# A table of expert tiles in two parts, the first worked out from seven of eight batches

## The reference

```python
def _L0_ffn_ref(hidden_states, router_w, router_b, w1, b1, w2, b2):   # E = 16 experts, K = 4
    logits = hidden_states @ router_w + router_b
    probs = jax.nn.softmax(logits, axis=-1)
    topw, topi = jax.lax.top_k(probs, K)
    topw = topw / jnp.sum(topw, axis=-1, keepdims=True)
    combine = jnp.sum(jax.nn.one_hot(topi, E) * topw[..., None], axis=2)
    ...
    def body(acc, expert):
        hmid = jax.nn.gelu(x @ w1e + b1e, approximate=False)          # w1e 256x512, w2e 512x256
        return (acc + (hmid @ w2e + b2e) * ce[:, None], None)
x = x + _L0_attn_ref(_layernorm(x), ...)
x = x + _L0_xattn_ref(_layernorm(x), ctx_1024, ctx_1024, ...)
x = x + _L0_ffn_ref(_layernorm(x), ...)
```

## Time and profile before

| what | value |
|---|---|
| median of 3 runs | 1757.58 us (1753.62 to 1761.1) |
| the profiled execution | 1751.44 us |
| its span, first to last instruction | 1749.4 us |
| mean granted TensorE clock | 0.968 of full speed |
| TensorE busy | 1597.4 us (91%) |
| VectorE, ScalarE, GpSimd busy | 1185.3, 1069.6, 505.0 us |
| the expert block starts, in the span | 1225.05 us |

### The profile page before, as it was taken

The page is one execution under the profiler, slowest core; times in us unless marked ns, Lnnn a source line. Parts: engine busy times, 40 slices in busy tenths (PEclk is TensorE's granted clock), DMA queues, the critical chain, the costliest instruction groups (busy, mean ns, idle before and its releaser), DMA issues. The chain is left out here.

```text
span 1749.4 us, 35493 instructions
## 1 busy us (share of the span) xinstructions
PE 1597.4 (91%) x12466; PEld 1341.6 (77%) x12466; DVE 1185.3 (68%) x2648; ACT 1069.6 (61%) x2698; POOL 505.0 (29%) x431
## 2 busy tenths in 40 slices
PE   5899889999999999999999999961699999999995
PEld 4888867677777776776777777741699999999995
DVE  6988856667677677776776776655566666666662
ACT  4555466666666566666666666642466666666663
POOL 2444400000301202103013021044155554554544
PEclk9999999999999999999999999985799999999997
DMA  3121110000100201101002001074577777877873
GB/s 96 37 85 73 37 61 1 1 25 1 64 25 14 75 1 45 45 1 65 25 6 84 1 29 36 1 256 166 155 163 181 173 175 176 177 179 164 188 171 46
DMA packets 92622, 144.52 MB, mean 83 GB/s; under 512 B 12272, under 2 KB 50720, under 8 KB 92448
## 3 DMA queue, kind: packets, MB, share of 16 engines
q1 hardware_dynamic: 61824, 101.40, 18.6%
q0 software_dynamic: 28896, 38.62, 12.2%
q10 hardware_dynamic: 1728, 2.23, 0.4%
HBM read 90.76 MB, written 51.46 MB: 81 GB/s over the span
## 5 line engine op out<-in xcount | busy, mean ns | idle before, releaser
L1193 ACT ACTIVATE xa_prob<-xa_S,xa_nmax 128x512 f32<-128x512 f32 (+3 forms) x512 | 266.5, 535 | 136.1 <-DVE xa_nmax L1303 124.8
L1710 POOL DMA_INDIRECT out<-ex_y,ex_x x158 | 254.6, 1611 | 262.7 <-ACT ex_y L1659 147.6
L1615 PE MATMUL ex_H<-ex_xT,ex_w 128*128 128x256 f32 x1896 | 247.3, 287 | 8.5 <-DVE ex_xT L1679 8.5
L1615 PEld LDWEIGHTS ex_H<-ex_xT,ex_w 128*128 128x128 f32 x1896 | 233.1, 192 | 8.9 <-issue 8.9
L1627 PE MATMUL ex_Y<-experts_w_hi,ex_hT 128*128 x1264 | 234.2, 279 | 0.0
L1515 POOL DMA_INDIRECT expert_rows<-xa_xn,xa_rows x128 | 127.8, 999 | 302.9 <-DVE xa_prob L1315 254.0
L1303 DVE TENSOR_REDUCE xa_nmax<-xa_S 128x2 f32<-128x1024 f32 (+3 forms) x256 | 198.1, 816 | 9.4 <-remote 8.2
L1627 PEld LDWEIGHTS ex_Y<-experts_w_hi,ex_hT 128*128 128x128 f32 x1264 | 198.9, 188 | 0.0
L1685 DVE TENSOR_TENSOR ex_hT<-ex_h,ex_hT 128x512 fp32r<-128x512 f32 x158 | 109.5, 694 | 122.7 <-ACT ex_hT L1652 87.5
L1207 ACT ACTIVATE xa_probT<-xa_work 128x512 f32<-128x512 f32 x256 | 140.0, 602 | 79.0 <-PE xa_work L1075 78.6
L1627 PE MATMUL ex_Y<-experts_w_lo,ex_hT 128*128 x632 | 176.8, 280 | 0.0
(11 more groups left out here) (312 smaller groups left out, 3583.8 us busy)
## 6 DMA issues: line engine op xcount, KB each, us to landing
ex_w_raw<-in_w SPq DMA_DIRECT2D x79, 512.0 KB
ex_x<-expert_rows SPq DMA_DIRECT2D x79, 273.0 KB
experts_w_lo<-in_w SPq DMA_DIRECT2D x4, 2048.0 KB, 9.7
expert_rows<-ahead_x SPq DMA_DIRECT2D x16, 273.0 KB
a_x<-in_x SPq DMA_DIRECT2D x8, 512.0 KB, 4.6
x_rows<-a_x_both SPq DMA_DIRECT2D x8, 512.0 KB, 5.4
ahead_ctx<-in_ctxT SPq DMA_DIRECT2D x8, 512.0 KB, 4.3
out<-xa_x SPq DMA_DIRECT2D x8, 512.0 KB
```

What stands on the lines that cost most here:

```text
L1193: m = act.activation(prob[n % 2][:, odd, PROB_AT[i]:PROB_AT[i] + width], SB[slot[at]][:, odd, col:col + width], ACT.Exp, bias=nmax[n % 2][ ...
L1615: m = pe.matmul(bank[:, (f % 2) * ROWS:(f % 2 + 1) * ROWS], ww[:, c, f * P:(f + 1) * P], xx[:, c, :], start=(i == 0), stop=(i == len(terms ...
L1710: pool.indirect_dma_start(out, bass.IndirectOffsetOnAxis(x_in[j % NX][:, a, ID:ID + 1].bitcast(I32), 0), y[j % NY][:, a, :], None, compute ...
```

## The change

The table is worked out in two parts. The first uses the counts of seven batches: only full tiles, and of them the first 41, a number that is there whatever the routing (`SURE_TILES`). It is computed in the last pair of the attention. The second holds the other 38 tiles and is computed in the expert block behind tile 4. Twelve of the last batch's sixteen scatters and the pads (now in halves) move into the expert block. x has five buffers instead of six, three of them tiles of the attention. The constants and buffers of the attention are kept through the expert block. The high parts of w2 are all made ahead of the output projection, and six of the low parts in the expert block.

```diff
+SURE_TILES = -(-((B - 1) * S * TOPK - E * (ROWS - 1)) // ROWS)
+LATE_TILES = MOE_TILES - SURE_TILES
@@ class Tables (new), part 0 and part 1
+    def work_out(self, dve, w, done, part, ahead, kept, count):
+        dve.memset(one, 1.0) ...
+        dve.tensor_scalar(self.scr_i[:], count[:], float(part * (ROWS - 1)), None, add)
+        ... shift right, to float; part 1: tiles = tiles - kept.used
+        ... scan, hit, owner, before; part 1 also some, behind, here, used (the tiles an expert has had)
+        dve.tensor_tensor(row, number[:], before, op=sub)
+        for back, meets in ((1, meets_1), (2, meets_2)):
+            dve.tensor_scalar(meets, row, float(back - 1), float(ADD_STEP), ALU.is_le, mult)
+        if part == 1: row = row + used
+        ... first row of the tile; part 0: kept.used = tiles of each expert, cut at SURE_TILES
+    def transpose(self, pe, w, done, bank, ident):
+        w.wait_ge(done, done.order[-5])
+        ... 4 transposes
+    def give_out(...): ... owner, first_row, landed of this part's tiles
@@ attention_plan
+        elif p == 7:
+            second.append(("tables", None))
...
-    plan += [*(("scatter", (b - 1, i, end, 1)) for i, _ in SCATTER_AT[1]), ("add_b2", (b - 1, 1)), *split_w2(0, 3),
-             ("output", (b, 1, 0)), *split_w2(3, 5), ("output", (b, 1, 1)), ("find3", b), ("norm3", b),
-             ("transpose_x3", (b, 0)), ("transpose_x3", (b, 1)), *split_w2(5, 9), ("route", b), ("choose", b), ("mark", b),
-             ("weigh_gates", b), ("place", b), *(("scatter", (b, i, end, 1)) for i in range(SCATTERS)),
-             ("tables", None), ("turn_gates", b), ("add_b2", (b, 0)), ("add_b2", (b, 1)), *split_w2(9, E)]
+    plan += [*(("scatter", (b - 1, i, end, 1)) for i, _ in SCATTER_AT[1]), ("add_b2", (b - 1, 1)),
+             *(("high_w2", e_) for e_ in range(E)), *low_w2(0, 3), ("output", (b, 1, 0)), *low_w2(3, 5), ("output", (b, 1, 1)),
+             ("first_loads", None), ("find3", b), ("norm3", b), ("transpose_x3", (b, 0)), ("transpose_x3", (b, 1)),
+             *low_w2(5, LOW_W2), ("route", b), ("choose", b), ("mark", b), ("weigh_gates", b), ("place", b), ("turn_gates", b),
+             *(("scatter", (b, i, end, 1)) for i in range(SCATTERS_FIRST)), ("add_b2", (b, 0)), ("add_b2", (b, 1))]
@@ cross_attention, sync
-                    ... 16 pad writes
+                elif step == "first_loads":
+                    w.wait_ge(t_dve, ("landed", 2))
+                    ... x and w1 of tiles 0 and 1 loaded by the first table
             w.wait_ge(x2_out, B - 1)
-            w.wait_ge(padded, E - 1)
+            for i, load in enumerate(first_in):
+                w.wait_ge(load, i % 2)
@@ cross_attention, gpsimd
-            w.wait_ge(scattered, (B - 1, *last_scatter))
@@ experts
-NX, NW = 6, 3
+NX, NW, FIRST = 5, 3, 2
-        x_in = [sb(f"x{i}", [P, RT, PAY]) for i in range(NX)]
+        x_in = [*kept.x_in, sb("x2", [P, RT, PAY]), xn3[:, 0:RT, :], xn3[:, RT:2 * RT, :]]
-        plan = [("load_x", j) for j in range(4)] + [("load_w1", j) for j in range(NW)]
-        plan += [("split_w1", 0), ("split_w1", 1), ("load_w1", NW), ("transpose", 0)]
+        plan = [("load_w1", 2), ("load_x", 2), ("split_w1", 0), ("transpose", 0), ("split_w1", 1), ("load_w1", 3), ("low_w2", None)]
         for j in range(MOE_TILES + 1):
+            plan += [("load_x", 3)] if j == 0 else []
             plan += [(step, at) for step, at in (("load_w1", j + 4), ("load_x", j + 4), ("transpose", j + 1), ("hidden", j),
                                                  ("split_w1", j + 2), ("results", j - 1)) if 0 <= at < MOE_TILES]
+            plan += [("tables", None)] if j == 4 else []
+            plan += [("pad", e_) for e_ in (2 * (j - 5), 2 * (j - 5) + 1) if 0 <= e_ < E]
@@ experts, sync
                 if step == "load_x":
+                    w.wait_ge(scattered[0], (B - 1, RT - 1, TOPK - 1), j == 3)
+                    w.wait_ge(scattered[1], last_scatter, j == 4)
+                    w.wait_ge(t_dve, ("landed", 2), j >= SURE_TILES)
+                    w.wait_ge(padded, (E - 1, RT - 1), j >= SURE_TILES)
                     w.wait_ge(t_pe, j - NX, j >= NX)
                     w.wait_ge(y_ev, j - NX, j >= NX)
-                    w.wait_ge(added[j % NY], (j - NX, RT - 1), j >= NX)
+                    w.wait_ge(added[(j - NX) % NY], (j - NX, RT - 1), j >= NX)
+                elif step == "pad":
+                    row = sp.value_load(pad_i[0:1, j:j + 1], min_val=0, max_val=E * REGION - ROWS)
+                    for a in range(RT):
+                        sp.dma_start(... half a pad ...)
@@ experts, tensor
+                if step == "tables":
+                    w.wait_ge(x_hi, 4)
+                    w.wait_ge(x_lo, 4)
+                    tables.transpose(pe, w, t_dve, XB[0], ident).then_inc(tables_pe.of(0), 1)
                 elif step == "transpose":
+                    w.wait_ge(t_dve, ("landed", 2), j == 6)
                 elif step == "results":
+                    w.wait_ge(low_w2, E - 1)
@@ experts, scalar
+            act.activation(warm[:], ahead.number[:], ACT.Gelu)
@@ experts, vector
+                if step == "low_w2":
+                    for e_ in range(LOW_W2, E):
+                        ... low part of w2 of expert e_
+                elif step == "tables":
+                    dve.tensor_tensor(pad_i[:], routing["count"][0:1, :], ahead.region[:], op=ALU.add)
+                    tables.work_out(dve, w, t_dve, 1, ahead, kept, routing["count"])
+                    w.wait_ge(tables_pe, 0)
+                    tables.give_out(dve, t_dve, 1, XB[0], ahead, routing)
@@ experts, gpsimd
-            ... ident
+            for i in range(SCATTERS_FIRST * ALL_ROWS // SCATTERS, ALL_ROWS):
+                ... the other twelve scatters
+            ... the pad's memset and iota
```

More of the change, by code:

```diff
@@ L791 @@
 PLACE = ("pos", "count", "key", "key_masked", "key8")
-TABLES = ("pad", "one", "tiles_up", "tiles_i", "tiles", "cum", "hit", "owner", "hit_tiles", "before", "some",
-          "owner_some", "row", "row_used", ("meets", 1), ("meets", 2), "row_up", "row_at", "row_past", "row_some", "owner_out", "row_out",
-          ("landed", 1), ("landed", 2))
 ROUTING = {"route": ROUTE, "choose": CHOOSE, "mark": MARK, "weigh_gates": WEIGH, "place": PLACE}
-SCATTERS, ALL_ROWS = 8, N_TILES * TOPK
+SCATTERS, ALL_ROWS, SCATTERS_FIRST = 8, N_TILES * TOPK, 2
 SCATTER_AT = {7: ((0, 3), (1, 2), (2, 1)), 0: ((3, 3), (4, 2), (5, 1)), 1: ((6, 3), (7, 2))}
@@ L886, in cross_attention @@
         pos = small("pos")
-        pads = x1[0][:].rearrange("p t c -> p (t c)")[:, 0:RT * PAY].rearrange("p (a c) -> p a c", c=PAY)
         gates, gatesT = sb("gates", [P, N_TILES, P], F32R), sb("gatesT", [P, S], F32R)
-        rows_i = [sb(f"rows{i}", [P, N_TILES, TOPK], I32) for i in range(2)]
+        rows_i = kept.rows_i
+        tables = Tables(sb, lg)
         heads = ExitStack()
@@ L944, in cross_attention @@
         lg_pe, pos_pe, tables_pe = signal("lg_pe", batches), signal("pos_pe", batches), signal("tables_pe", [0])
-        r_dve = signal("r_dve", [(at, n) for step, at in plan for n in ROUTING.get(step, ())] + list(TABLES))
+        r_dve = signal("r_dve", [(at, n) for step, at in plan for n in ROUTING.get(step, ())])
+        t_dve = signal("t_dve", Tables.of_part(0))
+        first_in = landed("first_x0", [0]), landed("first_x1", [1]), landed("first_w0", [0]), landed("first_w1", [1])
         r_act, r_rows = signal("r_act", batches), signal("r_rows", batches)
-        scattered = landed("scattered", [(b, t, k) for b in batches for t in range(N_TILES) for k in range(TOPK)])
-        padded = landed("padded", range(E))
+        scattered = landed("scattered", [(b, t, k) for b in batches[:-1] for t in range(N_TILES) for k in range(TOPK)])
+        scattered_last = [landed(f"scattered_last{u}", [(B - 1, t, k) for t in range(u * RT, (u + 1) * RT) for k in range(TOPK)])
+                          for u in range(N_TILES // RT)]
         last_scatter = (N_TILES - 1, TOPK - 1)
@@ L1429, in vector @@
                 elif step == "tables":
-                    tiles, cum, one, hit = (scr[:, i, :] for i in range(4))
-                    owner, before, row, some, meets_1, meets_2 = (of_tile[:, i:i + 1] for i in range(6))
-                    w.wait_ge(r_dve, (B - 1, "count"))
-                    dve.tensor_tensor(pad_i[:], count[0:1, :], region[:], op=ALU.add).then_inc(r_dve.of("pad"), 1)
-                    dve.memset(one, 1.0).then_inc(r_dve.of("one"), 1)
-                    dve.tensor_scalar(scr_i[:], count[:], float(ROWS - 1), None, ALU.add).then_inc(r_dve.of("tiles_up"), 1)
@@ L1481, in gpsimd @@
+                    tables.work_out(dve, w, t_dve, 0, ahead, kept, routing["count"])
+                    w.wait_ge(tables_pe, 0)
+                    tables.give_out(dve, t_dve, 0, bank(step, at), ahead, routing)
         def gpsimd(pool):
@@ L1526, in cross_attention, with experts @@
             block.sync(sync)
```

(11 more changed lines are left out.)

265 lines of the change are left out of this document (163 added, 102 removed).

## The result

| | before | after |
|---|---|---|
| median of 4 runs each, same chip | 1755.95 us | 1806.23 us (1796.25 to 1808.82) |
| the profiled execution | 1751.44 us | 1796.25 us |
| its span | 1749.4 us | 1794.5 us |

The ratio is 1.0273, with a 95% interval of 1.0234 to 1.0313: the change makes the kernel slower by 2.7%. Forecast were 1786.5, a range of 1759 to 1806 and a chance of 0.80 for slower. The direction was right; the cost was put too low. The measured ratio, taken on the 1757.58 that the forecast started from, is 1805.6: the very end of the range, and outside the 1773 to 1801 that the forecast gave its own mechanism. The medians differ by 50.3 and the spans of the two profiled executions by 45.1, where the prediction's sum was +29.

What follows compares the result with a forecast made beforehand. TensorE, busy 91% of the span, was taken as the bound. Seam -20, tiles 3 to 10 +13, 10 to 41 +12, 41 to 60 +14, 60 to 78 +8, end -2, pads +4: +29, 1786.5 us (1759 to 1806).

Steps and rivals of the forecast that it cites:

- The seam: Between attention and experts, to tile 3's transposes: the expert block starts earlier, in all -20 us (-28 to -13).
- Tiles 3 to 10: Early expert block: TensorE stands still 9.5 us for the second table behind tile 4; +13 us (+2 to +16).
- The pace of the ring: Expert stage: with five x buffers loads come late, 6.53 us a tile; tiles 10 to 41 +12 us (0 to +21).
- the three changes of expert: Tiles 10 to 41: each change of expert was given 0.6 us, five of them counted in that stretch.
- Tiles 41 to 78: Late expert stage: many first tiles of experts, then five-buffer pace; +14 us to tile 60, +8 us after.
- The chain through GpSimd: Tiles 41 to 60: an expert's first tile waits for earlier adds, 7.8 us a step, second tiles 3.7.
- 1: Expert stage: the five x buffers refill in time and cost nothing; -11 us, 1747 us; chance 0.09.
- 2: Expert stage: half the five-buffer cost, 6.27 us a tile; about 1760 us; chance 0.11.
- 4: Between attention and experts: something still holds block one, -5 us instead of -20; 1801 us; chance 0.03.
- 3: Expert stage: w1 loads also come late behind blocked x loads on SyncE, 6.8 us a tile; 1806 us; chance 0.05.

Runs made afterwards that it cites:

- e4: The changed kernel with TensorE's transposes for the second table issued a tile behind VectorE's steps, five x buffers: 1806.69 us, 1.0272 of the kernel before.
- e1: The kernel before with one edit, five x buffers instead of six: 1813.98 us, 1.0313 of the kernel before.
- e2: The changed kernel with a sixth x buffer from tile 20 on: 1771.66 us, 1.0079 of the kernel before.
- e5: The changed kernel with six x buffers from the first tile on: 1742.15 us, 0.9979 of the kernel before.
- e3: The changed kernel with the first table moved behind four of the last pair's eight turns, five x buffers: 1801.27 us, 1.0239 of the kernel before.
- e8: The changed kernel with the pad writes beside tiles 20 to 27 instead of 5 to 12, five x buffers: 1788.77 us, 1.0262 of the kernel before.
- e6: e5 with both table moves, those of e3 and e4, added: 1734.62 us, 0.9941 of the kernel before.
- e7: e6 with 17 sure tiles instead of 41: 1728.53 us, 0.9921 of the kernel before.

## Why the prediction was nearly right, point by point

**The seam** came out as forecast, -20.9 for -20, but by luck, as a sum of misses that cancel. The last pair and what follows, in the kernel after, against the earlier trace rows; TensorE, the four lines being the table's transposes, the weighing of the pair before, that of the last pair, and the output projection.

```profile
1154.68 1.01 PE L201 MATMUL xa_work<-ahead_ident,xa_of_tile 128*1 128x128 f32 x4 [7.07 <-DVE kept_used L196]
...
1155.62 3.28 PE L1196 MATMUL xa_work<-xa_probT,xa_v 128*64 128x512 f32 x16
...
1168.73 4.54 PE L1196 MATMUL xa_work<-xa_probT,xa_v 128*64 128x512 f32 x16 [6.47 <-ACT xa_probT L1310]
...
1174.95 0.55 PE L1213 MATMUL xa_work<-xa_Wo_hi,xa_oT_lo 128*128 128x256 f32 x1 [0.96 <-DVE xa_oT_lo L1436]
```

Count from the last pair's first scatter (1148.33 before, 1145.81 after), for the second profile had been 2.5 ahead already, which nothing in the change does. The first weighing is then 9.81 behind it instead of 1.62 ('s 1149.95): 8.2 late, and I had said 8.3. The last weighing is 12.9 late. Of the 8.3 I let 5 reach the block's end, and 11.7 did: the projection, at 1165.73 before, is 29.14 behind the scatter instead of 17.40. From the projection to block two it took 33.25 instead of 59.32, -26.1, where I had -23.3. Counted like this the block starts 14.3 earlier, not 18.3; tile 3 follows 21.34 behind it (23.5 forecast, 25.39 before), and 2.5 of drift make up the -20.9. Why the delay grew on its way is in the last section.

**Tiles 3 to 10:** the mechanism and its size were right. TensorE's line behind tile 4, with tiles 5 and 6 around it:

```profile
1242.04 0.66 PE L1681 MATMUL ex_X<-ahead_ident,kept_x 128*128 128x128 f32 x4
...
1253.86 1.01 PE L201 MATMUL ex_X<-ahead_ident,ex_of_tile 128*1 128x128 f32 x4 [5.42 <-DVE ex_of_tile L191]
1255.56 1.09 PE L1681 MATMUL ex_X<-ahead_ident,kept_x 128*128 128x128 f32 x4 [0.68 <-DVE routing_landed L210]
```

13.52 between two tiles is 7.4 over 6.1, and tile 6 then took 8.15, 2.0 more, as it began at the 0.50 clock; 9.5 were forecast for the standstill alone, so that this term fits is in part luck. e4 shows that this stood in for waits of the ring, so +11.2 is not 7.4 + 4 of separable causes.

**The pace of the ring is the step that failed.** It said that a turn g from first add to landed load is 11.0, that three tiles take 8.6 + g, and so one 6.53, with TensorE waiting 0.4 ahead of nearly every tile. The loop is the right one (e1, e2 and e5 show it, and the chain above has every link), but two of its sizes were low. First g. Over the loads of tiles 20 to 59 the first add stands 7.92 ahead of the load's issue and that 3.49 ahead of the transposes, 11.4 together. The 7.92 was to be had from the trace of before, whose mean over the same tiles is 7.93; I took one turn with 7.57, and went down another tenth in the belief that a slower stage loads the DMA engines less. The share did fall (between 20 and 41 from 0.77 before to 0.72 after), and the time from the add to the freed load did not. Second the tile itself, 6.24 in the loop instead of 6.11. With the 2.49 from the end of the results to the add, three tiles take 2.49 + 6.24 + 11.41 = 20.14, one 6.71. Over 20 to 41, 143.29/21 = 6.82 were measured; the 0.11 left is what I gave to the three changes of expert there (3 x 0.6 / 21 = 0.09). This holds for after's profiled execution; e3, e4 and e8 took 6.94 to 6.97 over the same tiles, and what adds the tenth wasn't told apart. And the waits come as one of 1.3 to 1.9 ahead of every third tile, since the loop ties tile j to j-3, not to j-1. As to the Trainium skill's formula for one DMA ("DMA: Bandwidth & Descriptors", Anatomy of one DMA), by which the turn was 7.6 and the ring free: the runs reject it here, with 11.4 for the same two DMAs and their issues. The section gives it for DMAs that GpSimd issues, as the adds are; the load is SyncE's.

**Tiles 41 to 78.** The chain through GpSimd is as forecast. First adds of tiles 43 to 47:

```profile
1535.97 1.55 POOL L1812 DMA_INDIRECT out<-ex_y,kept_xn  x1 [3.82 <-ACT ex_y L1743]
...
1543.71 1.55 POOL L1812 DMA_INDIRECT out<-ex_y,kept_xn  x1 [4.33 <-ACT ex_y L1743]
...
1551.39 1.84 POOL L1812 DMA_INDIRECT out<-ex_y,kept_x  x1 [4.27 <-POOLq L1808]
...
1559.30 2.06 POOL L1812 DMA_INDIRECT out<-ex_y,kept_x  x1 [4.07 <-POOLq L1808]
...
1567.01 1.63 POOL L1812 DMA_INDIRECT out<-ex_y,ex_x  x1 [3.79 <-POOLq L1808]
```

Steps of 7.7 to 7.9, as I had 7.8. Tile 41's first add to tile 60's took 135.6 instead of 131.8, because the second tile of an expert follows 4.1 to 4.6 behind, once 6.2, and not 3.7. The first five and the last thirteen tiles of the stretch to 78 had to go at the ring's true pace of about 6.8 and not at 6.53, which is 0.29 x 18 = 5.2 more. With the chain's 3.8 that is 9 of the 11.8 by which +22 fell short.

**The rivals.** 1 and 2 are refuted for this kernel by e1, 4 by the seam. For 3, w1 late as well, nothing is seen: no wait for a load of w1 stands in the groups of the transposes or the matmuls of x times w1. That its 1806 is the time measured is luck; the cause was another.

**What stays open:** an unhindered tile takes 6.18 to 6.25 in the changed kernel and 6.17 to 6.20 in e2 and e5, 6.10 to 6.12 before. The matmuls of `results` have a mean of 283 ns where before has 279 (groups by line); over 75 tiles it is some 5 us. e1 has 6.13 and 6.19 by turns. No run told its cause apart.

## What to carry to other kernels

A buffer ring is sized by one closed loop: add the durations from the buffer's last reader to its refilled state, mean over many turns, and compare with the ring's tiles at full pace; here the loop takes 20.1 us, six buffers give it four tiles (24.4, slack 4.3) and five give it three (18.3), and the 1.8 that are missing are paid again every three tiles. A wait that is taken away was worth nothing as long as a second loop stood just behind it (e4), or its time came back a few tiles later (e6); so open the tightest loop first (e5) and then count the others again (e7). Moving 20 us of work off a seam paid only after the buffer which it had cost was found elsewhere, and then little: 0.2% in e5, 0.8% with fewer sure tiles in e7.

## What the runs showed of the hardware that was not expected

From the last pair's first scatter to the output projection after took 8.4 us longer than e5, which runs the same instructions there. After's windows of 10 us from that scatter on, then those of e5; columns are stretch, us, busy by engine (PE, PEld, DVE, ACT, POOL), clock, DMA share, GB/s.

```profile
1145.81:1155.81 10.00, 1.73 (x8) 0.86 (x10) 6.33 (x29) 2.86 (x12) 7.54 (x8) 0.57 1.09 362
1155.81:1165.81 10.00, 5.76 (x36) 3.22 (x34) 1.18 (x5) 2.48 (x4) 7.56 (x9) 0.84 0.96 333
1165.81:1175.81 10.00, 6.12 (x22) 3.11 (x23) 1.75 (x3) 3.67 (x5) 0.33 (x1) 0.50 0.05 16
```

```profile
1137.98:1147.98 10.00, 1.63 (x8) 0.85 (x10) 6.33 (x29) 2.87 (x12) 7.54 (x8) 0.58 1.09 362
1147.98:1157.98 10.00, 8.55 (x54) 4.65 (x53) 1.39 (x6) 4.17 (x8) 7.56 (x9) 0.91 0.97 339
1157.98:1167.98 10.00, 5.99 (x48) 5.82 (x48) 8.95 (x12) 10.00 (x11) 0.33 (x1) 0.95 0.64 204
```

The hole of 7.1 us for the first table is in the first stretch of both, and both have the lower clock there (0.57, 0.58). It isn't what parts them: after was back at 1.00 between 1157.8 and 1163.8, as e5 was at the same distance from its scatter. They part at ScalarE's copies of the last pair, here after's, then e5's:

```profile
1162.40 0.60 ACT L1313 ACTIVATE xa_probT<-xa_work 128x512 f32<-128x512 f32 x1 [0.84 <-PE xa_work L1184]
...
1163.82 0.60 ACT L1313 ACTIVATE xa_probT<-xa_work 128x512 f32<-128x512 f32 x1 [0.83 <-remote]
...
1165.95 0.60 ACT L1313 ACTIVATE xa_probT<-xa_work 128x512 f32<-128x512 f32 x1 [1.53 <-remote]
1168.08 0.60 ACT L1310 ACTIVATE xa_probT<-xa_work 128x512 f32<-128x512 f32 x1 [1.53 <-remote]
```

```profile
1151.83 2.23 ACT L1315 ACTIVATE xa_probT<-xa_work 128x512 f32<-128x512 f32 x4
```

In after the last three each waited 0.83 to 1.53 us for something that the profile doesn't name (`remote`), though TensorE's transposes for them had ended at 1162.27. TensorE so stood still for 6.47 ahead of the last weighing, where e5 has 0.74. In this second hole the granted clock fell to 0.50, the 1.2 GHz level, and it stood there from 1164.8 to 1177.8; the 16 weighings took 4.54, in e5, at the upper level, 2.37. The last weighing starts 6.3 later and takes 2.2 longer, which makes up the 8.4.

The other profiles bear this out. From the first scatter to the projection e2 took 29.1 and e4 28.2, both with such waits of ScalarE, one after the other; e8 took 21.9 without one. With the first table moved behind four turns it was 24.3 in e3, with one wait of 5.84, and 17.7 in e6 and e7, without. The kernel before took 17.4 with one of 5.82, and e1, the same program there, 14.4 with one of 4.28. The six profiles with such waits are those of before, after and the first four runs; the four without are those of the last four runs, on the other chip. What ScalarE waits for stands on no row, and whether it is the chip or the execution that decides was not tried.
